# Newton-Schulz matrices turned by transposing DMA transfers in place of TensorE transposes, every third new X evicted by VectorE

## The chip, the cores and the metric

One core of a Trainium2 chip runs the whole program. The metric is the device time in microseconds (us) of one execution. TensorE (PE in the profile) multiplies and, in this kernel, also transposes; VectorE (DVE), ScalarE (ACT) and GpSimd (POOL) do the elementwise work, the first two also bring results out of PSUM; SyncE (SP) issues most DMA transfers.

## The reference, cut to what matters

A transformer layer on 8 batches of 256 tokens with 256 features: a modulated layer norm, an attention part whose three small weights per head are updated by one gradient step, and a mixture of 16 experts. The change is in the update. For each batch and each of two heads there are three 128x128 gradients, 48 matrices in all, and each is made nearly orthogonal by five Newton-Schulz steps in bf16:

```
def _zeropower_ns5(G):
    X = G.astype(jnp.bfloat16)
    nrm = jnp.linalg.norm(X.astype(jnp.float32).reshape(X.shape[0], -1), axis=1)
    X = X / (nrm[:, None, None].astype(jnp.bfloat16) + 1e-07)
    for a, b, c in NS_COEFFS:
        A = X @ jnp.swapaxes(X, 1, 2)
        Bm = b * A + c * (A @ A)
        X = a * X + Bm @ X
    return X.astype(jnp.float32)
```

The result is added to the gradient, its rows are scaled, and the sum is the weight with which the tokens' outputs are computed.

## The kernel before

Each engine has its own program, written out by hand in the order in which it runs; semaphores (`S[...]`) tell the engines of each other's progress, and a wait holds up everything behind it on its engine.

The 48 matrices lie in `X`, `[128, 48, 128]` bf16, and are taken in 12 groups of four (`NGRP`, `MPG`). Five steps over 12 groups make 60 turns, n = 0 to 59. A product X X^T needs the transposed X as TensorE's operand, so there is a second array `XT` of the same shape. The stage is a software pipeline, one loop over rounds r on each engine. In round r

- TensorE does A for turn r (L893, from `XT`), A A for turn r - 1 (L904, from `Ar`), the new X for turn r - 2 (L917 and L918, from `X`, `aI` and `Br`) and the transposes of the new X for turn r - 3 (L933);
- ScalarE evicts A scaled by b to `Ar` (L617) and the new X to `X` (L626);
- VectorE makes `Br` = b A + c A A (L1300) and copies the transposed matrices from PSUM to `XT` (L1306).

`Ar`, `Br` and the PSUM banks of A, A A, X and the transposes are two deep each. Turn n of one step and turn n + 12 of the next are the same group.

Before the first step there is no new X to turn. `first_turn(g)` (L857) transposes the 12 normalised groups on TensorE and `first_turned` (L571 on ScalarE for the even groups, L1263 on VectorE for the odd ones) copies them; groups 0 to 2 stand before the gradient products of the last batch, groups 3 to 5 behind them, and the rest in the rounds that `TURN_AT` names. The normalisation `x_init(b)` (L1257, L1259) of a batch's six matrices hangs on a chain: gradients out of PSUM (L578), cast to bf16 (L1251), sums of squares (L586, L1284, L1286), a sum over partitions on TensorE (L844), its copy (L566), a square root on GpSimd (L405, L407). For batch 7, the last, it stands in VectorE's round 6.

In the last step GpSimd adds each new X to its gradient (L460), TensorE transposes the sum (L949) and VectorE copies it (L1311).

SyncE starts the loads of the first five blocks of expert weights (`raw`, L329, two buffers) when the gradients are done; GpSimd splits each in two (L449, L451), beginning when all of `X` is normalised. From about 285 us on the mixture runs, in which nothing changes.

Of the kernel before, what the change touches and what calls it, by code (L numbers as in the profile page):

```python
# [27 lines left out]
P = 128  # L28
# [46 lines left out]
def build(nc, x_d, c_d, wmod_d, qkvw_d, w02_d, w1_d, wnat_d, wo_d, onw_d, gate_d, ident_d, moew_d, comb_d, out_d):  # L75
    ctx = ExitStack()
    with ctx:
# [149 lines left out]
        def bank(i):  # L227
# [16 lines left out]
            "f_ps", "f_sum", "f_norm", "f_b", "f_inv", "x_init", "t0_ps", "t0_a", "t0_v", "t_ps", "t_sb", "a_ps", "a_sb", "b_ps", "b_sb", "x_ps", "x_sb",  # L244
# [28 lines left out]
        def xt_ps(m):  # L273
            return bank(6 + m % 2).bitcast(BF16)[:, 0:BLK].rearrange("p (a d) -> p a d", d=P)

        FIRST_T = [4, 5, 2, 3, 4, 5, 6, 7, 6, 7, 6, 7]
        TURN_AT = {0: 6, 1: 7, 2: 8, 5: 9, 8: 10, 9: 11}

        def first_xt_ps(g):
            return bank(FIRST_T[g]).bitcast(BF16)[:, 0:BLK].rearrange("p (a d) -> p a d", d=P)  # L280
# [35 lines left out]
        def _(sp):  # L316
# [8 lines left out]
            sp.wait_ge(S["dw_ps"], B)  # L325
# [5 lines left out]
            for j in range(CPG):  # L331
                weights(j)
# [27 lines left out]
        def _(po):  # L360
# [96 lines left out]
            for g in range(NGRP):  # L457
                po.wait_ge(S["x_sb"], NGRP * (NS_STEPS - 1) + g + 1)
                wv = dw[:, g * MPG:(g + 1) * MPG, :]
                po.tensor_tensor(wv, wv, X[:, g * MPG:(g + 1) * MPG, :], ALU.add).then_inc(S["w_ok"], 1)  # L460
# [31 lines left out]
        def _(ac):  # L492
# [75 lines left out]
            def first_turned(g):  # L568

                ac.wait_ge(S["t0_ps"], g + 1)  # L570
                ac.activation(XT[:, g * MPG:(g + 1) * MPG, :], first_xt_ps(g), ACT.Copy).then_inc(S["t0_a"], 1)  # L571

# [32 lines left out]
            for g in (0, 2):  # L605
                first_turned(g)
# [3 lines left out]
            first_turned(4)  # L610
            for r in range(NGRP * NS_STEPS + 2):
# [6 lines left out]
                if TURN_AT.get(r - 1, 1) % 2 == 0:  # L618
                    first_turned(TURN_AT[r - 1])
# [92 lines left out]
        def _(pe_):  # L712
# [133 lines left out]
            def first_turn(g):  # L846

                pe_.wait_ge(S["x_init"], (4 * g + 3) // 6 + 1)
                for before in range(g):
                    if FIRST_T[before] == FIRST_T[g]:  # L850
                        pe_.wait_ge(S["t0_v" if before % 2 else "t0_a"], before // 2 + 1)
                if g == 6:
                    pe_.wait_ge(S["dw_sb"], NH * B)
                elif g >= 9:
                    pe_.wait_ge(S["t_sb"], {9: 2, 10: 5, 11: 6}[g])
                for a in range(MPG):
                    last = pe_.transpose(first_xt_ps(g)[:, a, :], X[:, g * MPG + a, :], identb[:, :])  # L857
                last.then_inc(S["t0_ps"], 1)

            pe_.wait_ge(S["const"], 7 + NS_STEPS)  # L860
            for b in range(1, B + 1):
# [7 lines left out]
                if b == B:  # L869
                    pe_.wait_ge(S["b_dg"], B)  # L870
                    for g in range(3):
                        first_turn(g)
# [3 lines left out]
            for g in range(3, 6):  # L876
                first_turn(g)
            NR = NGRP * NS_STEPS
            for r in range(NR + 4):
                n = r  # L880
                if n < NR:
                    g = n % NGRP
                    if n >= NGRP:
                        pe_.wait_ge(S["t_sb"], n + 1 - NGRP)
                    else:
                        pe_.wait_ge(S["t0_v" if n % 2 else "t0_a"], n // 2 + 1)
# [9 lines left out]
                if 0 <= n < NR:  # L896
# [3 lines left out]
                    else:  # L900
                        pe_.wait_ge(S["t0_v" if n else "t0_a"], 2)
# [5 lines left out]
                if 0 <= n < NR:  # L907
                    g = n % NGRP
                    pe_.wait_ge(S["b_sb"], n + 1)
                    if n >= 2:  # L910
                        pe_.wait_ge(S["x_sb"], n - 1)
                    else:
                        pe_.wait_ge(S["t0_v" if n else "t0_a"], 3)
# [6 lines left out]
                n = r - 3  # L920
                if 0 <= n < NR - NGRP:
                    g, m = n % NGRP, NGRP + n
                    pe_.wait_ge(S["x_sb"], n + 1)
                    if n >= 2:
                        pe_.wait_ge(S["t_sb"], n - 1)
                    if n in (0, 6):
                        pe_.wait_ge(S["t0_a"], 5 if n == 0 else 6)
                    elif n in (1, 3, 7):
                        if n == 1:
                            pe_.wait_ge(S["f_sum"], B)  # L930
                        pe_.wait_ge(S["t0_v"], {1: 4, 3: 5, 7: 6}[n])
                    for a in range(MPG):
                        last = pe_.transpose(xt_ps(m)[:, a, :], X[:, g * MPG + a, :], identb[:, :])  # L933
                    last.then_inc(S["t_ps"], 1)
                if r in TURN_AT:
                    first_turn(TURN_AT[r])
                if r == 2:
                    pe_.wait_ge(S["t0_v"], 4)
                    frob_sums(B - 1)
                n = r - 4  # L940
                if n >= NR - NGRP:
# [4 lines left out]
                    else:  # L946
                        pe_.wait_ge(S["t_sb"], NR - NGRP)
# [5 lines left out]
            pe_.wait_ge(S["x_sb"], NR)  # L953
# [131 lines left out]
        def _(ve):  # L1085
# [175 lines left out]
            def first_turned(g):  # L1261
                ve.wait_ge(S["t0_ps"], g + 1)
                ve.tensor_copy(XT[:, g * MPG:(g + 1) * MPG, :], first_xt_ps(g)).then_inc(S["t0_v"], 1)  # L1263

# [12 lines left out]
            first_turned(1)  # L1277
# [3 lines left out]
            first_turned(3)  # L1281
# [243 lines left out]
```

## Time and profile before

| | |
|---|---|
| runs | 711.73, 716.71, 719.69 us |
| median | 716.71 us |
| profiled execution | 712.38 us |
| its span in the trace | 710.6 us |
| mean granted TensorE clock | 0.983 |
| busy: PE, DVE, ACT, POOL | 94%, 68%, 49%, 30% of the span |

The span runs from the first instruction to the last one. A busy time is the sum over one engine's instructions; matmuls overlap, so the distance between the starts of two of them says more than the duration of one. In a timeline each row gives the start, the duration and the instruction, with its line, and in brackets the idle time before it and who ended that.

### The profile page before, as it was taken

What the parts mean: (1) busy time and instruction counts of PE and PEld (TensorE: products, weight loads), DVE (VectorE), ACT (ScalarE), POOL (GpSimd) and SP (SyncE); (2) the same over time, 40 slices, a digit from 0 to 9 for tenths busy, and PEclk for the clock granted to TensorE, in tenths of its full rate; (3) what the DMA queues carried; (4) which work ended last, traced back from release to release, by engine and by line L of the source; (5) the groups of instructions that cost most, each with busy time, mean ns of one, the idle gap of its engine ahead of it and who ended that gap; (6) DMA issues with size and microseconds to landing.
All of it is one profiled execution on the core that took longest, in us unless ns stands there. A gap on an engine that the chain in (4) does not pass through costs nothing.

```text
span 710.6 us, 11547 instructions
## 1 busy us (share of the span) xinstructions
PE 665.6 (94%) x4132; PEld 568.1 (80%) x4132; DVE 483.3 (68%) x960; ACT 345.2 (49%) x746; POOL 212.3 (30%) x210
## 2 busy tenths in 40 slices
PE   3998889779997899998999999999999999999997
PEld 3778779779995688887888888888888888888885
DVE  4788888999995478767545675665754766655555
ACT  3367669879998976453322323323223223223222
POOL 2255867944037664134100330013200331000000
PEclk9999999999998899999999999999999999999999
DMA  8000000021000000032003432243212432121223
GB/s 315 1 0 1 2 1 1 1 68 48 3 3 2 0 1 1 0 118 92 30 15 83 118 104 72 63 108 112 85 60 76 117 118 69 60 69 59 66 72 122
DMA packets 20472, 41.48 MB, mean 58 GB/s; under 512 B 3360, under 2 KB 3616, under 8 KB 20288
## 3 DMA queue, kind: packets, MB, share of 16 engines
q1 hardware_dynamic: 19392, 37.65, 17.2%
q10 hardware_dynamic: 832, 2.43, 1.0%
q8 instruction: 34, 0.56, 0.4%
q0 software_dynamic: 192, 0.66, 0.2%
q14 instruction: 22, 0.18, 0.1%
HBM read 38.50 MB, written 2.23 MB: 57 GB/s over the span
## 4 chain that ended last, share of the span: by engine, by line
PE 73%; ACT 9%; DVE 9%; POOL 3%; issue 3%; DMA 2%; ACTq 0%; DVEq 0%; POOLq 0%
PE ps L987 36%; PE ps L1058 18%; ACT junk L634 3%; PE ps L804 3%; PE ps L917 2%; PE ps L893 2%; PE ps L918 2%; PE ps L904 2%; PE ps L933 2%; DMA qkvw<-in_qkvw 1%; PE ps L834 1%; ACT junk L586 1%; PE ps L1005 1%; PE ps L1024 1%; DVE sq L1172 1%
## 5 line engine op out<-in xcount | busy, mean ns | idle before, releaser
L705 ACT ACTIVATE sgm<-ps,zero 128x512 f32<-128x512 f32 x100 | 68.9, 690 | 268.7 <-PE ps L987 268.7
L987 PE MATMUL ps<-h2hi,whi 128*128 128x512 f32 x400 | 156.1, 390 | 0.0
L987 PE MATMUL ps<-h2lo,whi 128*128 128x512 f32 x400 | 155.6, 389 | 0.0
L987 PE MATMUL ps<-h2hi,wlo 128*128 128x512 f32 x400 | 155.6, 389 | 0.0
L1466 DVE TENSOR_TENSOR am<-sgm,ps 128x512 f32<-128x512 f32 x88 | 60.6, 688 | 138.6 <-ACT sgm L705 138.5
L449 POOL CAST whi<-raw 128x768 fp32r<-128x768 f32 x25 | 22.4, 895 | 239.2 <-DMA raw<-in_moew 236.7
L987 PEld LDWEIGHTS ps<-h2lo,whi 128*128 128x128 f32 x400 | 75.1, 188 | 15.7
L987 PEld LDWEIGHTS ps<-h2hi,whi 128*128 128x128 f32 x400 | 75.1, 188 | 15.5
L987 PEld LDWEIGHTS ps<-h2hi,wlo 128*128 128x128 f32 x400 | 75.1, 188 | 15.4
L1058 PE MATMUL ps<-ahi,whi 128*128 128x512 f32 x200 | 77.9, 390 | 0.1
L1058 PE MATMUL ps<-alo,whi 128*128 128x512 f32 x200 | 77.8, 389 | 0.0
L1058 PE MATMUL ps<-ahi,wlo 128*128 128x512 f32 x200 | 77.8, 389 | 0.0
L1475 DVE TENSOR_TENSOR pm<-am,cw 128x512 f32<-128x512 f32 x88 | 72.2, 821 | 6.4 <-DMA cw<-combine 4.0
L1430 DVE TENSOR_TENSOR alo<-pm,ahi 128x512 fp32r<-128x512 f32 x100 | 75.7, 757 | 0.2
L695 ACT ACTIVATE ahi<-pm 128x512 fp32r<-128x512 f32 x100 | 62.3, 623 | 7.8 <-DVE pm L1468 5.0
L451 POOL TENSOR_TENSOR wlo<-raw,whi 128x768 fp32r<-128x768 f32 x25 | 47.9, 1917 | 2.0
L1058 PEld LDWEIGHTS ps<-ahi,whi 128*128 128x128 f32 x200 | 37.5, 188 | 8.3 <-DVE alo L1430 0.5
L1058 PEld LDWEIGHTS ps<-alo,whi 128*128 128x128 f32 x200 | 37.5, 188 | 7.8
L1058 PEld LDWEIGHTS ps<-ahi,wlo 128*128 128x128 f32 x200 | 37.5, 188 | 7.7
L1300 DVE SCALAR_TENSOR_TENSOR Br<-ps,Ar 128x512 bf16<-128x512 f32 x60 | 41.5, 691 | 2.5 <-PE ps L904 1.2
L617 ACT ACTIVATE Ar<-ps 128x512 bf16<-128x512 f32 x60 | 35.4, 593 | 4.1 <-PE ps L893 1.8
L626 ACT ACTIVATE X<-ps 128x512 bf16<-128x512 f32 x60 | 35.9, 598 | 3.1 <-PE ps L918 1.0
(206 smaller groups left out, 1238.5 us busy)
## 6 DMA issues: line engine op xcount, KB each, us to landing
raw<-in_moew SPq DMA_DIRECT2D x25, 384.0 KB, 3.8
cw<-combine SPq DMA_DIRECT2D x32, 256.0 KB, 3.2
cw<-combine SPq DMA_DIRECT2D x16, 224.0 KB, 3.0
cw<-combine SPq DMA_DIRECT2D x16, 192.0 KB, 2.9
cw<-combine SPq DMA_DIRECT2D x16, 160.0 KB, 2.7
cw<-combine SPq DMA_DIRECT2D x16, 128.0 KB, 3.0
out<-x1T SPq DMA_DIRECT2D x8, 256.0 KB, 3.7
cw<-combine SPq DMA_DIRECT2D x16, 96.0 KB, 2.8
```

The source lines that it names most:

```text
L449: po.tensor_copy(whi[wg % 2][:, c, :], raw[:, j % 2, :]).then_inc(S["w_hi"], 1)
L451: po.tensor_tensor(wlo[wg % 2][:, c, :], raw[:, j % 2, :], whi[wg % 2][:, c, :].bitcast(F32), ALU.subtract).then_inc(S["w_prep"], 1)
L617: ac.activation(Ar[:, n % 2, :], bank(n % 2), ACT.Copy, scale=NS[n // NGRP][1]).then_inc(S["a_sb"], 1)
L626: ac.activation(X[:, g * MPG:(g + 1) * MPG, :], bank(4 + n % 2).rearrange("p (a d) -> p a d", d=P), ACT.Copy).then_inc(S["x_sb"], 1)
L695: ac.activation(ahi[:, n % 4, :], pm[:, n % 3, :], ACT.Copy).then_inc(S["e_hi"], 1)
L705: ac.activation(sgm[:, n % 2, :], gate_bank(n), ACT.Silu, bias=zero[:, :]).then_inc(S["e_sg"], 1)
L987: last = mm(o, w_, a_[:, kc, tok], start=(kc == 0 and k == 0), stop=(kc == KC - 1 and k == 2))
L1058: last = mm(bank(6 + f), w_, a_, start=(c == 0 and k == 0), stop=(c == CPG - 1 and k == 2))
L1300: ve.scalar_tensor_tensor(out=Br[:, n % 2, :], in0=bank(2 + n % 2), scalar=c_ / (b_ * b_), in1=Ar[:, n % 2, :], op0=ALU.mult, op1=ALU.add) ...
L1430: ve.tensor_tensor(alo[:, n % 3, :], pm[:, n % 3, :], ahi[:, n % 4, :].bitcast(F32), ALU.subtract).then_inc(S["e_lo"], 1)
L1466: ve.tensor_tensor(am[:, n % 2, :], sgm[:, n % 2, :], lin_bank(n), ALU.mult).then_inc(S["e_a"], 1)
L1475: ve.tensor_tensor(pm[:, n % 3, :], am[:, n % 2, :], cw[:, k % 3, :], ALU.mult).then_inc(S["e_p"], 1)
```

## The change

The transposes of X leave TensorE, and their copies leave ScalarE and VectorE. SyncE issues, for each of the 60 turns, one transposing DMA transfer of a group from `X` to `XT`, 128 KB. Before it SyncE waits for the transfer four turns back, for the normalised X (first step) or for A of the turn 12 back and the eviction of its new X (later steps). TensorE waits for the transfer before A. The loads of the raw weights are issued between transfers 4, 8, 20, 24 and 28. In the first four steps the new X of every third turn is evicted by VectorE in place of ScalarE (`on_vector`); `evicted(n)` names the semaphore and count of turn n. The normalisations of batches 6 and 7 stand in VectorE's rounds 2 and 5 in place of 3 and 6.

```diff
+        NTURN = NGRP * NS_STEPS
+
+        def on_vector(n):
+            return n % 3 == 2 and n < NGRP * (NS_STEPS - 1)
+
+        def evicted(n):
+            if on_vector(n):
+                return S["x_sb_v"], sum(on_vector(k) for k in range(n + 1))
+            return S["x_sb_a"], sum(not on_vector(k) for k in range(n + 1))
+
+        def turned_in(m):
+            return S[f"xt_ld{m % 4}"], 16 * (m // 4 + 1)
...
-            sp.wait_ge(S["dw_ps"], B)
+            sp.wait_ge(S["dw_ps"], B - 1)
+            sp.wait_ge(S["b_dg"], B)
...
-            for j in range(CPG):
-                weights(j)
+            for m in range(NTURN):
+                g = m % NGRP
+                if m >= 4:
+                    sp.wait_ge(*turned_in(m - 4))
+                if m < NGRP:
+                    sp.wait_ge(S["x_init"], (4 * g + 3) // 6 + 1)
+                else:
+                    sp.wait_ge(S["a_ps"], m - NGRP + 1)
+                    sp.wait_ge(*evicted(m - NGRP))
+                sp.dma_start_transpose(XT[:, g * MPG:(g + 1) * MPG, :], X[:, g * MPG:(g + 1) * MPG, :]).then_inc(turned_in(m)[0], 16)
+                if m in (4, 8, 20, 24, 28):
+                    if m == 4:
+                        sp.wait_ge(S["dw_ps"], B)
+                    weights((4, 8, 20, 24, 28).index(m))
...
-                if n >= 0:
+                if n >= 0 and not on_vector(n):
                     g = n % NGRP
                     ac.wait_ge(S["x_ps"], n + 1)
                     ac.activation(X[:, g * MPG:(g + 1) * MPG, :], bank(4 + n % 2).rearrange("p (a d) -> p a d", d=P),
-                                  ACT.Copy).then_inc(S["x_sb"], 1)
+                                  ACT.Copy).then_inc(S["x_sb_a"], 1)
...
+                    pe_.wait_ge(*turned_in(n))
                     if n >= NGRP:
-                        pe_.wait_ge(S["t_sb"], n + 1 - NGRP)
+                        pe_.wait_ge(*evicted(n - NGRP))
...
-                n = r - 3
-                if 0 <= n < NR - NGRP:
-                    g, m = n % NGRP, NGRP + n
-                    pe_.wait_ge(S["x_sb"], n + 1)
-                    if n >= 2:
-                        pe_.wait_ge(S["t_sb"], n - 1)
...
-                    for a in range(MPG):
-                        last = pe_.transpose(xt_ps(m)[:, a, :], X[:, g * MPG + a, :], identb[:, :])
-                    last.then_inc(S["t_ps"], 1)
-                if r in TURN_AT:
-                    first_turn(TURN_AT[r])
...
-                if r in (3, 6):
-                    x_init(B - 2 if r == 3 else B - 1)
+                if r in (2, 5):
+                    x_init(B - 2 if r == 2 else B - 1)
...
-                n = r - 3
-                if 0 <= n < NR - NGRP:
-                    g, m = n % NGRP, NGRP + n
-                    ve.wait_ge(S["t_ps"], n + 1)
-                    ve.tensor_copy(XT[:, g * MPG:(g + 1) * MPG, :], xt_ps(m)).then_inc(S["t_sb"], 1)
+                n = r - 2
+                if 0 <= n < NR and on_vector(n):
+                    g = n % NGRP
+                    ve.wait_ge(S["x_ps"], n + 1)
+                    ve.tensor_copy(X[:, g * MPG:(g + 1) * MPG, :], bank(4 + n % 2).rearrange("p (a d) -> p a d", d=P)).then_inc(S["x_sb_v"], 1)
```

How it moves SyncE's queue, from the last load of the start on (`gatew`, the router's weights). Before:

```order
7 L323 DMA gatew<-in_gate 128x32
8 L329 DMA raw<-in_moew 128x768 [waits dw_ps]
9 L329 DMA raw<-in_moew 128x768
10 L329 DMA raw<-in_moew 128x768 [waits w_prep] x3
11 L339 DMA combine<-combT 16x1024 [waits combT_ok]
```

And of the change, up to the first transfer of the second step:

```order
7 L327 DMA gatew<-in_gate 128x32
8 L345 DMA_TRANSPOSE XT<-X 128x4x128 [waits x_init,b_dg,dw_ps]
9 L345 DMA_TRANSPOSE XT<-X 128x4x128 [waits x_init] x3
10 L345 DMA_TRANSPOSE XT<-X 128x4x128 [waits x_init,xt_ld0]
11 L334 DMA raw<-in_moew 128x768 [waits dw_ps]
12 L345 DMA_TRANSPOSE XT<-X 128x4x128 [waits x_init,xt_ld1]
13 L345 DMA_TRANSPOSE XT<-X 128x4x128 [waits x_init,xt_ld2]
14 L345 DMA_TRANSPOSE XT<-X 128x4x128 [waits x_init,xt_ld3]
15 L345 DMA_TRANSPOSE XT<-X 128x4x128 [waits x_init,xt_ld0]
16 L334 DMA raw<-in_moew 128x768
```

The first load of raw weights now has five transfers before it in the queue, and the second nine.

VectorE at the start of the stage, from the first Br. Before:

```order
215 L1300 SCALAR_TENSOR_TENSOR Br<-ps,Ar 128x512 [waits b_ps]
216 L1263 COPY XT<-ps 128x512 [waits t0_ps]
217 L1300 SCALAR_TENSOR_TENSOR Br<-ps,Ar 128x512 [waits b_ps]
218 L1257 RECIPROCAL finv<-fnb 128x6 [waits f_b]
219 L1259 TENSOR_TENSOR X<-X,finv 128x768 [waits f_inv]
220 L1300 SCALAR_TENSOR_TENSOR Br<-ps,Ar 128x512 [waits x_ps,b_ps]
221 L1306 COPY XT<-ps 128x512 [waits t_ps]
```

And of the change, from the same place into the steady part:

```order
212 L1260 SCALAR_TENSOR_TENSOR Br<-ps,Ar 128x512 [waits b_ps]
213 L1226 RECIPROCAL finv<-fnb 128x6 [waits f_b]
214 L1228 TENSOR_TENSOR X<-X,finv 128x768 [waits f_inv]
215 L1260 SCALAR_TENSOR_TENSOR Br<-ps,Ar 128x512 [waits b_ps]
216 L1260 SCALAR_TENSOR_TENSOR Br<-ps,Ar 128x512 [waits x_ps,b_ps] x2
217 L1266 CAST X<-ps 128x512 [waits x_ps]
218 L1226 RECIPROCAL finv<-fnb 128x6 [waits f_b]
219 L1228 TENSOR_TENSOR X<-X,finv 128x768 [waits f_inv]
220 L1260 SCALAR_TENSOR_TENSOR Br<-ps,Ar 128x512 [waits x_ps,b_ps] x3
221 L1266 CAST X<-ps 128x512 [waits x_ps]
```

The copies to `XT` are gone, the scaling of batch 6 stands before the second Br, and one eviction of X (CAST) stands behind every third Br.

## Rows read from the trace of the kernel before

**Rows 1.** The page, busy time, share of the span and instructions of each engine.

```profile
PE 665.6 (94%) x4132; PEld 568.1 (80%) x4132; DVE 483.3 (68%) x960; ACT 345.2 (49%) x746; POOL 212.3 (30%) x210
```

**Rows 2.** Stretches: from:to, length, busy time (instructions) by engine, PEclk, DMA.

```profile
137.00:143.60 6.60, 5.95 (x49) 5.76 (x50) 5.85 (x12) 4.90 (x17) 4.81 (x6) 0.74 0.01 2
...
159.30:205.00 45.70, 45.70 (x823) 45.70 (x821) 44.77 (x83) 43.95 (x81) 7.99 (x7) 1.00 0.08 20
```

**Rows 3.** Groups of instructions by line, whole span: busy us, mean ns, idle before.

```profile
L1306 DVE COPY XT<-ps 128x512 bf16<-128x512 bf16 x48 | 20.3, 424 | 1.1 <-PE ps L933 1.1
...
L933 PE MATMUL ps<-identb,X 128*128 128x128 bf16 x192 | 18.5, 219 | 2.1 <-ACT XT L571 1.2 <-DVE XT L1263 0.9
...
L460 POOL TENSOR_TENSOR dw<-dw,X 128x512 f32<-128x512 f32 x12 | 13.7, 1160 | 38.2 <-ACT X L626 38.1
```

**Rows 4.** Timeline of PE, one steady round: start, duration, instruction.

```profile
161.56 0.39 PE L893 MATMUL ps<-XT 128*128 128x128 bf16 x4
...
162.45 0.39 PE L933 MATMUL ps<-identb,X 128*128 128x128 bf16 x4
162.67 0.39 PE L893 MATMUL ps<-XT 128*128 128x128 bf16 x4
162.90 0.39 PE L904 MATMUL ps<-Ar 128*128 128x128 bf16 x4
```

**Rows 5.** Timelines of ACT and DVE, the same round.

```profile
161.53 0.60 ACT L626 ACTIVATE X<-ps 128x512 bf16<-128x512 f32 x1
162.03 0.59 ACT L617 ACTIVATE Ar<-ps 128x512 bf16<-128x512 f32 x1
162.65 0.60 ACT L626 ACTIVATE X<-ps 128x512 bf16<-128x512 f32 x1
...
163.32 0.69 DVE L1300 SCALAR_TENSOR_TENSOR Br<-ps,Ar 128x512 bf16<-128x512 f32 x1
```

**Rows 6.** Timeline of PE, end of the stage.

```profile
205.10 0.39 PE L893 MATMUL ps<-XT 128*128 128x128 bf16 x4
...
206.00 0.39 PE L893 MATMUL ps<-XT 128*128 128x128 bf16 x4
...
212.81 0.39 PE L893 MATMUL ps<-XT 128*128 128x128 bf16 x4
...
215.48 0.39 PE L893 MATMUL ps<-XT 128*128 128x128 bf16 x4
```

**Rows 7.** Timelines of PE, DVE and POOL, start of the stage.

```profile
137.60 1.46 PE L857 MATMUL ps<-identb,X 128*128 128x128 bf16 x12 [1.22 <-DVE dgb L1272]
...
150.47 0.22 PE L917 MATMUL ps<-X,aI 128*128 128x128 bf16 x1
...
159.32 0.39 PE L893 MATMUL ps<-XT 128*128 128x128 bf16 x4
...
143.76 0.55 DVE L1251 CAST X<-dw 128x768 bf16<-128x768 f32 x1
...
146.21 0.42 DVE L1263 COPY XT<-ps 128x512 bf16<-128x512 bf16 x1
146.54 0.68 DVE L1300 SCALAR_TENSOR_TENSOR Br<-ps,Ar 128x512 bf16<-128x512 f32 x1
...
148.28 0.96 DVE L1259 TENSOR_TENSOR X<-X,finv 128x768 bf16<-128x768 bf16 x1
...
149.81 1.35 POOL L405 TENSOR_TENSOR fnb<-fsum,half 128x6 bf16<-128x6 f32 x1 [3.96 <-ACT fsum L566]
151.25 0.24 POOL L407 TENSOR_SCALAR fnb<-fnb 128x6 bf16<-128x6 bf16 x1
```

**Rows 8.** The page, DMA issues: count, KB each, median us from issue to landing.

```profile
combine<-combT SPq DMA_DIRECT2D x2, 64.0 KB, 2.3
```

**Rows 9.** Timeline of SyncE's queue: start, time to issue.

```profile
142.74 0.81 SPq L329 DMA_DIRECT2D raw<-in_moew  x2
...
304.16 0.34 SPq L339 DMA_DIRECT2D combine<-combT  x1
```

**Rows 10.** DMA queues from 1.4 to 2.6 us: packets, MB, share of 16 engines.

```profile
q1 hardware_dynamic: 144, 0.01, 7.1%
```

**Rows 11.** The same from 16.5 to 17.6 us.

```profile
q1 hardware_dynamic: 312, 0.18, 54.0%
```

More of the change, by code:

```diff
@@ L242, in build @@
             "xb_ok", "f_ss", "g_sq", "f_s7",
-            "f_ps", "f_sum", "f_norm", "f_b", "f_inv", "x_init", "t0_ps", "t0_a", "t0_v", "t_ps", "t_sb", "a_ps", "a_sb", "b_ps", "b_sb", "x_ps", "x_sb",
+            "f_ps", "f_sum", "f_norm", "f_b", "f_inv", "x_init", "xt_ld0", "xt_ld1", "xt_ld2", "xt_ld3", "a_ps", "a_sb", "b_ps", "b_sb", "x_ps", "x_sb_a", "x_sb_v",
             "w_ok", "wt_ps", "wt_sb", "rss_ok", "ws_chain", "w_scale",
@@ L457, in _ @@
             for g in range(NGRP):
-                po.wait_ge(S["x_sb"], NGRP * (NS_STEPS - 1) + g + 1)
+                po.wait_ge(*evicted(NGRP * (NS_STEPS - 1) + g))
                 wv = dw[:, g * MPG:(g + 1) * MPG, :]
@@ L566, in sum_out @@
                 ac.activation(fsum[:, 6 * b:6 * b + 6], frob_ps(b), ACT.Copy).then_inc(S["f_sum"], 1)
-            def first_turned(g):
-                ac.wait_ge(S["t0_ps"], g + 1)
-                ac.activation(XT[:, g * MPG:(g + 1) * MPG, :], first_xt_ps(g), ACT.Copy).then_inc(S["t0_a"], 1)
             def grads_out(b):
@@ L604, in _ @@
             sum_out(B - 3)
-            for g in (0, 2):
-                first_turned(g)
             grad_squares(B - 2)
@@ L844, in frob_sums @@
                 mm(frob_ps(b), ones[:, :], fss[:, 6 * b:6 * b + 6], start=True, stop=True).then_inc(S["f_ps"], 1)
[L846 to L855, printed above, removed]
-                for a in range(MPG):
-                    last = pe_.transpose(first_xt_ps(g)[:, a, :], X[:, g * MPG + a, :], identb[:, :])
-                last.then_inc(S["t0_ps"], 1)
             pe_.wait_ge(S["const"], 7 + NS_STEPS)
@@ L870, in _ @@
                     pe_.wait_ge(S["b_dg"], B)
-                    for g in range(3):
-                        first_turn(g)
                     pe_.wait_ge(S["f_sum"], B - 2)
@@ L875, in _ @@
             frob_sums(B - 2)
-            for g in range(3, 6):
-                first_turn(g)
             NR = NGRP * NS_STEPS
@@ L910, in _ @@
                     if n >= 2:
-                        pe_.wait_ge(S["x_sb"], n - 1)
-                    else:
-                        pe_.wait_ge(S["t0_v" if n else "t0_a"], 3)
+                        pe_.wait_ge(*evicted(n - 2))
                     for a in range(MPG):
@@ L919, in _ @@
                     last.then_inc(S["x_ps"], 1)
-                n = r - 3
-                if 0 <= n < NR - NGRP:
-                    g, m = n % NGRP, NGRP + n
-                    pe_.wait_ge(S["x_sb"], n + 1)
-                    if n >= 2:
-                        pe_.wait_ge(S["t_sb"], n - 1)
[L926 to L932, printed above, removed]
-                        last = pe_.transpose(xt_ps(m)[:, a, :], X[:, g * MPG + a, :], identb[:, :])
-                    last.then_inc(S["t_ps"], 1)
-                if r in TURN_AT:
-                    first_turn(TURN_AT[r])
                 if r == 2:
-                    pe_.wait_ge(S["t0_v"], 4)
+                    pe_.wait_ge(S["dw_sb"], NH * B)
                     frob_sums(B - 1)
@@ L946, in _ @@
                     else:
-                        pe_.wait_ge(S["t_sb"], NR - NGRP)
+                        pe_.wait_ge(S["f_sum"], B)
                     for a in range(MPG):
@@ L950, in _ @@
                     last.then_inc(S["wt_ps"], 1)
-            pe_.wait_ge(S["x_sb"], NR)
+            pe_.wait_ge(*evicted(NR - 1))
             pe_.wait_ge(S["wt_sb"], NGRP)
@@ L1280, in _ @@
             x_init(B - 3)
-            first_turned(3)
             cast_grads(B - 1)
```

20 lines of the change are left out of this document (1 added, 19 removed).

## The prediction, made before the changed kernel ran

> **What bounds the kernel now.** I read the busy times first: TensorE (PE) is busy 94% of the 710.6 us [rows 1], so only what shortens PE's own sequence, or the waits in it, can pay. Then the table of stretches, for the place that the change touches: the Newton-Schulz stage runs from 143.6 to 219 us. In its steady part PE is busy for the whole 45.70 us, but VectorE (DVE) has 44.77 and ScalarE (ACT) 43.95 of the same stretch [rows 2]. Three engines are nearly full at once, so what comes off PE alone is not the gain.
>
> Then the timeline of one steady round, a round being one turn of the loop over 60 groups of four matrices. The product A = X X^T of one round starts at 161.56, the next at 162.67: the round takes 1.115 us [rows 4]. It has 20 matmuls 0.056 us apart: four transposes (L933), four for A (L893), four for A A (L904), eight for the new X (L917, L918). PE never waits in it.
>
> **What the change takes away in a steady round.** The four transposes start at 162.45 and the next group follows at 162.67: 0.22 us of PE per group, for the 48 groups of L933 [rows 3, 4]. VectorE's copies of the turned matrices go too, 48 of 424 ns [rows 3]. Every third new X moves from ScalarE (about 0.60 us each, row of 162.65 [rows 5]) to VectorE. The trace has no VectorE copy of this kind; the nearest row is its own operation Br, also 128x512 fp32 from PSUM to bf16, 0.69 us [rows 5]. I take 0.69. PE's sum for a round becomes 1.115 - 0.22 = 0.89 us. The row that shows such a round: the first one after the last transposes runs from 205.10 to 206.00, 0.90 us [rows 6].
>
> **Why the round won't become 0.89.** The buffers are two deep and the chain between the engines takes over. ScalarE evicts X and A in turns. An X eviction starts 0.20 us after the next group on PE does (162.45 to 162.65), and ScalarE's following operation starts no less than 0.50 us after it (161.53 to 162.03) [rows 4, 5]. So in the new order the eviction of A starts 0.70 after A's first matmul, runs 0.59 and hands over in about 0.05: A A can start at 1.34. PE would be there after one whole round and the four matmuls of the next A, at 0.89 + 0.22 = 1.11. The stall s counts twice on the way, once in each round: 1.11 + 2s = 1.34, s = 0.115, round = 1.005 us. Where VectorE takes X, ScalarE is free and this stall goes, but Br then waits for that copy (it would start at 0.20 + 0.60 = 0.80 instead of 0.22 + 0.42 = 0.64, the 0.42 from 162.90 to 163.32 [rows 4, 5]). It ends at 1.49 and the next X is late by about 0.2. So the third that is moved exchanges one stall for another of the same size. I take 1.00 us for a round, with 0.89 and 1.06 as its ends: the sum of PE alone, and both stalls in full in every third round. From round 10 (159.32) to the last with a transpose there are 41 rounds: 41 x (1.115 - 1.00) = 4.7 us.
>
> **The start of the stage.** Today the first 12 groups are turned by PE too (L857), twelve matmuls of them, 1.46 us from 137.60, ahead of the last gradient products [rows 7]. The transfers take their place beside the gradients. Part of that gain is lost, since PE begins cold there (granted clock 0.74 from 137 to 143.6, nearer to the lower level than what follows at 1.00 [rows 2]) and the gradients take over the slow matmuls: I take 0.9. The cast at 143.76, on which the last batch's norm hangs, moves up with it, and one copy (0.42 us each, 0.34 from start to start) between it and the first Br goes: Br at 145.3 instead of 146.54 [rows 7]. The scaling of batch 6 now stands a round earlier, in front of the second Br (0.96 us for the product that starts at 148.28, 1.15 with its reciprocal; it delayed the third Br before). By this the third X product starts at about 148.6 instead of 150.47, 1.9 us earlier [rows 7]. The scaling of batch 7 hangs on GpSimd, which starts its power at 149.81 now, 1.35 and 0.24 us long; it would start at 148.4, and 1.35 + 0.24 + 1.15 later, at 151.1, VectorE would go on. Then four rounds of 1.00 to round 10 at 155.3, against 159.32: 4.0 us in all [rows 7]. The last two transfers of the first pass leave at 151.1 and have four rounds to land.
>
> **The end.** For the last 12 groups PE has transposes of the sum (L949): 1.34 us a round (two from 212.81 to 215.48), with an addition of 1.16 on GpSimd [rows 3, 6]. Nothing there gets shorter or longer, since no X goes to VectorE in that step. The loads of raw weights that move between the transfers feed GpSimd's split, which now ends near 169; the latest would be issued by round 18 or so, near 163, as now. I cost them at nothing: the first user of the weights starts at 285.5 us.
>
> **What the transfers cost.** 60 of 128 KB each, SBUF to SBUF, on SyncE's queue, at most four in flight. There is none in the trace. Three prices are wanted.
> - Landing. The nearest row, 64 KB out of SBUF, lands in 2.3 us [rows 8]; with twice the bytes I allow 3.2. From X's eviction to the A that needs the transfer are 12 - 3 = 9 rounds, 9 us: hidden, unless it lands later than 9 us. But four in flight give one in landing / 4: 0.58 to 0.80 us, below 1.00. It begins to cost at 4 us.
> - The engines' time. If the rows of 256 bytes are packets of their own, there are 512. Small packets took 7.1% of 16 engines' 1.2 us over 144 of them, 9.5 ns each [rows 10], and 54.0% of 1.1 us over 312, 30 ns, these of about 580 bytes [rows 11]. Between them by size, some 20 ns: 512 x 20 / 16 = 0.64 us a group, 0.30 at 9.5 and 0.96 at 30.
> - The issue. SyncE takes 0.34 us for a plain one [rows 9].
>
> I take 0.64, which is below the round, so transfers cost the path nothing. Their upper end is from the same rows: four in flight and 30 ns gives 0.96, still covered; if a transfer holds the stream until it has landed, 2.3 us, it is not. With an interval I above 1.1 us the stream sets the end: 60 I + 2 us from 137.6, against 215.5 today for the last A [rows 6], a change of 60 I - 76 us. It breaks even near 1.27.
>
> **Sum.** 4.7 + 4.0 = 8.7 us off the profiled execution's 712.38 us: 703.7. That execution stands 4.3 below the median of 716.71, whose runs lie between 711.73 and 719.69; on the median's scale 708.
>
> **Rivals.**
> 1. *The stream of transfers is slower than the rounds.* Nothing in the trace shows how fast SyncE issues a transposing transfer or the engines move one. At I = 1.5 us the change is 60 x 1.5 - 76 = +14, 726 (731 on the median's scale); at 2.0 +44, 756 (761). For it: all prices above are of plain transfers. Against it: even the 30 ns packet leaves 0.96. It decides from 1.27 on; chance 0.21. The Trainium skill, "DMA: Bandwidth & Descriptors", in the table of transposes before the fast path, counts 262,144 sequencer cycles for 8,192 tiles from SBUF to SBUF, one push per tile; the X-bar section of the same page takes 16 partitions by 128 elements as one tile. By it the 32 tiles of a group are 1,024 cycles, an estimate of 0.85 us at 1.2 GHz ahead of any fixed part, and the sum stays as it is only if that part is under 0.3 us. No row here shows it.
> 2. *Transfers pass one after the other*, each occupying the stream for its whole landing time. With the 2.3 us of [rows 8]: 60 x 2.3 - 76 = +62, 774 (779). For it: no row shows two transposing transfers under way together. Against it: plain ones do overlap, as the two raw loads issued at 142.74 and 0.4 us later [rows 9]. Chance 0.16. The Trainium skill, "VectorE: DVE Perf Modes", section "The three transpose paths", gives 1309 ns for one 128x128 matrix by DMA against 390 on TensorE; four in a row would be an estimate of 5.2 us a group and 240 us lost. The same skill's "DMA: Bandwidth & Descriptors", section "Latency and other measured facts", has 261 GB/s for such transfers, 0.50 us a group, and would leave my sum.
> 3. *Nearly even*: an interval between 1.1 and 1.3, from landing in 4.5 to 5 us with four in flight or from issue. The gain of the start stays, that of the rounds goes: 60 x 1.2 - 76 = -4, to +2; about 709 to 714 (713 to 719). Chance 0.15.
> 4. The forecast, 0.48. Within it the change can do less than it says, because the round falls to 1.06 and not to 1.00 (41 x 0.06 = 2.5 less); that leaves 6 us, under 1%: 0.10 of the 0.48.
>
> One per cent is 7.2 us, about what the spread of the runs lets one tell. So faster 0.38, within 1% 0.10 + 0.15 = 0.25, slower 0.21 + 0.16 = 0.37. The range: 41 rounds at 0.95 and two us more at the start give about 703 on the median's scale, a low run 699. Its upper end takes in rival 1 to I = 2.0, 760, and leaves out rival 2. If the forecast's mechanism holds, its own range is 699 to 712.
>
> **What would show it.** The distance of two A products in the steady part: 1.00 confirms the chain, 0.89 says that I overcharged it, 1.2 or more with PE idle before A and a transfer as its releaser is rival 1. Their time to landing tells rival 2 (I = landing / 4 when they overlap, I = landing when not). The first Br near 145.3 and round 10 near 155.3 confirm the start. My sum is wrong if PE's idle time before A names a transfer anywhere after round 10.

## The result, and the profile after

The change makes the kernel slower: 729.44 us (median of 4, 727.66 to 732.53) against 714.22 (4, 711.43 to 719.69) in the same session, ratio 1.021 (1.018 to 1.025). The forecast was 708. The profiled execution has a span of 727.6 us against 710.6, 17.0 more. Measured on one scale, from the end of the last gradient product on VectorE to the last product A, the Newton-Schulz stage takes 92.5 us (139.5 to 232.0) instead of 77.9 (137.6 to 215.5): 14.6 of the 17.0. Another 1.9 is a later begin of the stage in code that the change doesn't touch. That begin lies between 137.3 and 143.8 us from one profiled run to another, also in kernels with the same code up to there, so the experiments below are compared by the length of the stage as well as by total time. A length comes from one profiled execution and is itself good to about 1.5 us: two runs below whose streams hold the same transfers and loads differ from the changed kernel by 1.0 and 1.4.

The stretches of the changed kernel, with the columns of [rows 2]:

```profile
137.00:143.60 6.60, 4.40 (x20) 4.37 (x21) 5.62 (x10) 4.00 (x17) 6.36 (x6) 0.58 0.22 44
143.60:160.00 16.40, 13.45 (x152) 12.28 (x151) 12.49 (x20) 9.29 (x19) 7.68 (x9) 0.75 0.90 128
160.00:200.00 40.00, 29.20 (x435) 25.79 (x432) 23.93 (x37) 25.69 (x47) 9.18 (x7) 0.96 0.67 117
200.00:232.00 32.00, 25.47 (x381) 22.70 (x382) 21.30 (x34) 23.08 (x40) 9.04 (x8) 1.00 0.54 92
```

Where [rows 2] has three engines full in the steady part, none is: PE is busy 29.2 of 40 us, VectorE 23.9, ScalarE 25.7, and the DMA engines 0.67. The page of the profile says what PE waits for; its groups have the columns of [rows 3]. The first line is the chain of work that ended last: 7% of the span runs through SyncE's queue (SPq), which had no part in it before:

```profile
PE 68%; ACT 8%; DVE 7%; SPq 7%; POOL 3%; issue 3%; DMA 3%; ACTq 0%; DVEq 0%; POOLq 0%
...
L883 PE MATMUL ps<-XT 128*128 128x128 bf16 x240 | 24.7, 228 | 17.9 <-DMA XT<-X 17.0
```

PE stands idle 17.9 us before A (L883), 17.0 of them for a transfer from `X` to `XT`. The prediction said that its sum is wrong if just this is seen. The products A on PE's timeline, to be held against [rows 4]:

```profile
196.16 0.40 PE L883 MATMUL ps<-XT 128*128 128x128 bf16 x4 [0.39 <-DMA XT<-X]
197.54 0.40 PE L883 MATMUL ps<-XT 128*128 128x128 bf16 x4 [0.31 <-DMA XT<-X]
198.86 0.40 PE L883 MATMUL ps<-XT 128*128 128x128 bf16 x4 [0.26 <-DMA XT<-X]
200.16 0.40 PE L883 MATMUL ps<-XT 128*128 128x128 bf16 x4 [0.23 <-DMA XT<-X]
201.44 0.40 PE L883 MATMUL ps<-XT 128*128 128x128 bf16 x4 [0.22 <-DMA XT<-X]
202.77 0.40 PE L883 MATMUL ps<-XT 128*128 128x128 bf16 x4 [0.26 <-DMA XT<-X]
```

A round takes 1.31 us, not 1.00 and not 1.115, and each A is released by a transfer. What sets the 1.31 stands on the timeline of SyncE's queue (start, time to issue):

```profile
196.38 1.21 SPq L345 DMA_TRANSPOSE XT<-X  x1
197.69 1.21 SPq L345 DMA_TRANSPOSE XT<-X  x1
...
202.93 1.92 SPq L345 DMA_TRANSPOSE XT<-X  x1
...
212.81 1.75 SPq L345 DMA_TRANSPOSE XT<-X  x1
...
222.51 2.13 SPq L345 DMA_TRANSPOSE XT<-X  x1
```

SyncE needs 1.21 us to issue one transposing transfer and 0.10 more to the next: 1.31. The plain transfer that the prediction took as its price needs 0.34 [rows 9]. Landing is not the limit. From 196 to 200 us the view of the queues gives

```profile
q1 hardware_dynamic: 1632, 0.39, 48.4%
...
XT<-X SPq DMA_TRANSPOSE x4, 2.4
```

that is 2.4 us to land (median), and 1,632 packets, three transfers of 544. They took 48.4% of 16 engines' 4 us, 19 ns a packet. Over the whole stage the median to land is 2.5 us; two transfers are under way at once.

**The 89.1 us of the stream.** The first issue is at 139.54, the last of 60 at 228.67. 59 intervals of 1.31 are 77.3; five loads of raw weights stand between them, 4.4; one wait for the scaling of batch 7, 1.3; and eight issues take 1.6 to 2.2 us instead of 1.21 (three are shown), which makes 6.1 with a gap of 0.5 us that follows one of them. Together 89.1. The last A is 3.3 us behind the last issue. So the stage ends when the stream ends, and it is late by the stream's four parts.

### The profile page after: what moved, and what is told of

Same layout as the page of the kernel before. It is cut to its first block, busy times and chain, and to the rows that moved or that the text cites. A ratio compares the mean times of both kernels' runs of the same rounds, so it can differ in the third digit from the quotient of the medians.

```text
span 727.6 us, 11064 instructions
## 1 busy us (share of the span) xinstructions
PE 664.8 (91%) x3892; PEld 561.0 (77%) x3892; DVE 471.4 (65%) x922; ACT 336.1 (46%) x724; POOL 212.2 (29%) x210
## 3 DMA queue, kind: packets, MB, share of 16 engines
q10 hardware_dynamic: 832, 2.43, 1.0%
## 4 chain that ended last, share of the span: by engine, by line
PE 68%; ACT 8%; DVE 7%; SPq 7%; POOL 3%; issue 3%; DMA 3%; ACTq 0%; DVEq 0%; POOLq 0%
PE ps L956 37%; PE ps L1027 18%; SPq L345 7%; ACT junk L641 2%; PE ps L811 2%; PE ps L841 2%; DMA qkvw<-in_qkvw 1%; PE ps L993 1%; ACT junk L598 1%; DMA XT<-X 1%; PE ps L974 1%; DVE x L1375 1%; PE ps L767 1%; DVE sq L1141 1%; DVE qk L1115 1%
## 5 line engine op out<-in xcount | busy, mean ns | idle before, releaser
L1027 PE MATMUL ps<-ahi,whi 128*128 128x512 f32 x200 | 77.9, 390 | 0.1
L883 PE MATMUL ps<-XT 128*128 128x128 bf16 x240 | 24.7, 228 | 17.9 <-DMA XT<-X 17.0
```

The lines of the kernel that those rows point to most:

```text
L883: last = mm(bank(n % 2)[:, a * P:(a + 1) * P], XTm, XTm, start=True, stop=True)
L1027: last = mm(bank(6 + f), w_, a_, start=(c == 0 and k == 0), stop=(c == CPG - 1 and k == 2))
```

## The experiments

Each is a change of the changed kernel if nothing else is said. "Interval" is the distance of two issues on SyncE, "stage" the length as defined above (before 77.9, changed 92.5). A ratio is to the kernel before, with its 95% interval.

### What sets the interval: the transfers in flight, their bytes, or the issue

**Eight in flight.** There are four more semaphores, and SyncE waits for the transfer eight back instead of four.

```
-            return S[f"xt_ld{m % 4}"], 16 * (m // 4 + 1)
+            return S[f"xt_ld{m % 8}"], 16 * (m // 8 + 1)
...
-                if m >= 4:
-                    sp.wait_ge(*turned_in(m - 4))
+                if m >= 8:
+                    sp.wait_ge(*turned_in(m - 8))
```

> Transfers may run eight deep in place of four. Theory A (SyncE's issue of a transposing transfer, 1.21 us and 0.10 between two, sets the interval): nothing changes, 1.31 us between two issues in the steady part, 726 to 732 us. Rival B (landing time with four in flight, 2.5 us and up to 5.0): the stops in the queue go, and the time falls by 5 to 10 us, to 719 to 725.

730.56 us, 1.024 (1.015 to 1.032); stage 91.1. The interval stays where it was:

```profile
191.08 1.21 SPq L345 DMA_TRANSPOSE XT<-X  x1
192.39 1.21 SPq L345 DMA_TRANSPOSE XT<-X  x1
```

The number of transfers in flight is not the limit.

**The same bytes without the turn.** The 48 later transfers are plain copies to a spare tile `XD`. A reads what the 12 first turns left, so the products are of stale matrices.

```
+                if m < NGRP:
+                    sp.dma_start_transpose(XT[...], X[...])...
+                else:
+                    sp.dma_start(XD[:, m % 4 * MPG:(m % 4 + 1) * MPG, :], X[...])...
...
```

> From the second step on the 48 transfers are plain copies of the same 128 KB from SBUF to SBUF into a ring of four, waited for in the same way, and A is made from the matrices turned for the first step (later steps don't use their own transposed X). Theory A: the issue falls to 0.3 to 0.6 us, the interval is set by the rounds (about 1.0 us), and the time is 708 to 714 us. Rival C (what costs is 128 KB through the DMA engines from SBUF to SBUF, or the chain of waits A, eviction, transfer, A): the interval stays at 1.3 and the time near 729.

711.99 us in the one run, where the kernel before has a median of 715.19 (9 runs); stage 72.5. SyncE takes 0.46 to 0.55 us for 42 of the 48 and 1.0 to 2.1 for six (the distance below is set by the rounds now):

```profile
191.41 0.52 SPq L349 DMA_DIRECT2D XD<-X  x1
192.57 0.46 SPq L349 DMA_DIRECT2D XD<-X  x1
```

and the rounds take 1.04 on average. As many transfers with as many bytes and the same waits are hidden as soon as they don't transpose.

**Half the bytes.** Each transfer turns two of its four matrices, and A uses each of them twice, so half of the products are of the wrong matrix.

```
-  sp.dma_start_transpose(XT[:, g * MPG:(g + 1) * MPG, :], X[:, g * MPG:(g + 1) * MPG, :])
+  sp.dma_start_transpose(XT[:, g * MPG:g * MPG + 2, :], X[:, g * MPG:g * MPG + 2, :])
...
-                        XTm = XT[:, g * MPG + a, :]
+                        XTm = XT[:, g * MPG + a % 2, :]
```

> Each transfer turns two of a group's four matrices, and A uses these two twice (the other two A are left out). If an issue has a fixed price (A1): still 1.2 to 1.3 us each, 726 to 732 us. If the price goes with the bytes or blocks (A2): about 0.65 to 0.75 us an issue, less than a round, and 706 to 713 us.

727.06 us, 1.019 (1.010 to 1.027); stage 89.1:

```profile
192.04 1.17 SPq L345 DMA_TRANSPOSE XT<-X  x1
193.31 1.19 SPq L345 DMA_TRANSPOSE XT<-X  x1
```

Half the bytes, almost the same issue. So the price is one per transfer, and nearly none per byte.

**Twice the bytes, half the transfers.** 30 transfers of two groups (256 KB), which each wait for the second group's eviction.

```
-            for m in range(NTURN):
+            for k in range(NTURN // 2):
+                m = 2 * k
...
-  sp.dma_start_transpose(XT[:, g * MPG:(g + 1) * MPG, :], X[:, g * MPG:(g + 1) * MPG, :])
+  sp.dma_start_transpose(XT[:, g * MPG:(g + 2) * MPG, :], X[:, g * MPG:(g + 2) * MPG, :])
```

> 30 transfers of eight matrices in place of 60 of four. A1 (fixed price per issue): 30 issues of 1.3 us, hidden, 706 to 713 us. A2 (price by blocks): 2.4 us an issue, 30 gaps of 0.10 saved, and a later start of each pair: 725 to 733 us.

709.45 us (8 runs), 0.992 (0.989 to 0.995); stage 73.9, 4.0 shorter than before and 18.6 shorter than in the changed kernel.

```profile
187.56 1.23 SPq L347 DMA_TRANSPOSE XT<-X  x1
189.58 1.23 SPq L347 DMA_TRANSPOSE XT<-X  x1
```

Twice the bytes, 1.23 us to issue: the sizes 64, 128 and 256 KB give medians of 1.19, 1.21 and 1.23. The rounds pace the stream, and from 160 to 200 us PE's weight loads wait for a transfer once (the view of waits: us in all, times, the longest):

```profile
PEld ps L885 <- DMA XT<-X: 1.2, 1, 1.2
```

This one edit turns the loss into a gain, which shows the cause of the largest part. No run issued the transfers from another engine, so whether part of the price is SyncE's own is open.

### The other parts of the stream

**The raw weights from GpSimd's own queue.** Takes the five loads out of SyncE's stream.

```
-                if m in (4, 8, 20, 24, 28):
-                    ...
-                    weights((4, 8, 20, 24, 28).index(m))
...
+            def load_raw(j):
+                ...
+                po.dma_start(raw[:, j % 2, :], moew_d[:, j, :]).then_inc(S[f"ld_rp{j % 2}"], 16)
...
```

> The five loads of raw weights leave SyncE's queue: GpSimd issues them itself. Theory A (everything that SyncE issues adds up, since its queue is the bottleneck): 60 transfers stay 1.31 us apart, and the 4.4 us that the loads take between them (0.6 to 1.8 each) come off: ratio to before 1.013 to 1.017 in place of 1.021. Rival (the loads hide in the queue's waits, or cost by traffic on the DMA engines, which stays): no change, 1.019 to 1.025.

726.65 us, 1.018 (1.014 to 1.023); stage 90.7. Of 4.4 us only 1.9 come back, between what the two expectations say. Long issues took a part of the rest: those at 156.28, 168.00 and 175.01 us take 2.43, 2.47 and 2.09. The loads' 4.4 is what they occupy in the stream; that taking them out is worth 4.4 was not shown, and 1.9 is hardly more than the 1.4 by which "eight in flight" was shorter with all loads in place.

**One wait less.** SyncE doesn't wait for A's signal, since X's eviction implies it.

```
-                    sp.wait_ge(S["a_ps"], m - NGRP + 1)
```

> The changed kernel without SyncE's wait for A before each later transfer (the eviction of the new X, which comes after that A, is still waited for): one instruction less per transfer in SyncE's queue. If the price of an issue were in the waits, the interval of 1.31 us would fall by about 0.1 and the time by 5 us; if it is the transposing transfer's own, it stays at 1.30 to 1.31. The long issues (1.6 to 2.4 us, every seventh or eighth) come at wider spacing if they go with the number of instructions read, at the same if with time or transfers. Total 724 to 731 us.

729.31 us, 1.020 (1.015 to 1.024), stage 91.5, interval 1.31, and the long issues at the same distance of about 10 us. The 0.10 between two issues is not that wait.

**The long issues.** In the changed kernel the queue of instructions q8 moves nine packets of 16 KB from 137 to 232 us (count, MB, share):

```profile
q8 instruction: 9, 0.15, 0.7%
```

Read in windows of half a microsecond, the first eight lie at 149.0, 159.0, 167.5, 178.0, 190.5, 202.5, 212.5 and 222.0 us, and SyncE's long issues start at 149.41, 158.50, 167.58, 178.31 (a raw load, 1.77 us instead of 0.57), 191.31, 202.93, 212.81 and 222.51. (The eighth long transfer of the sum above, 1.58 us at 164.59, has its packet on the other queue of instructions, q14, at 164.0; the raw load's excess is in the 4.4.) The distance of about 10 us could be that of PE's instructions, of which it has 32 a round (16 matmuls and 16 weight loads), far more than any other engine. Two edits change their number. First, two matrices share one matmul of 256 columns, so PE has the same columns with half the instructions (half of the products are then of a matrix with its neighbour):

```
-                    for a in range(MPG):
-                        XTm = XT[:, g * MPG + a, :]
-                        last = mm(bank(n % 2)[:, a * P:(a + 1) * P], XTm, XTm, start=True, stop=True)
+                    for a in range(0, MPG, 2):
+                        last = mm(bank(n % 2)[:, a * P:(a + 2) * P], XT[:, g * MPG + a, :],
+                                  XT[:, g * MPG + a:g * MPG + a + 2, :]..., start=True, stop=True)
...
```

> Asked: where the long issues of the transfers come from (eight of 1.6 to 2.2 us in the changed kernel instead of 1.21, 6.1 us in all). In the changed kernel each of these eight has a transfer of instructions on queue q8 (one packet of 16 KB) in the same half microsecond, 149.0 to 222.0 us, nine to twelve us apart; the three on q14 go with shorter delays. Here two matrices share one matmul of 256 columns in A, A A and the new X: the same columns on TensorE, half the instructions (8 matmuls and 8 weight loads a round instead of 16 and 16). Half of the products are of one matrix with its neighbour, so the output is not the reference's. If the long issues come with the fetch of TensorE's instructions: four or five of them with q8, twice as far apart, the stage about 3 us shorter, ratio to the kernel before about 1.017 (1.012 to 1.019). If they belong to the transfers themselves (every seventh or eighth issue, whatever TensorE does): eight again at the same distance, ratio 1.021 (1.018 to 1.025).

726.45 us, 1.017 (1.013 to 1.020); stage 90.0, 2.5 shorter. The interval of the ratio overlaps with the changed kernel's (1.018 to 1.025), and equal streams differ by 1.4, so these two numbers don't decide. The trace does. It has five packets on q8 in the same stretch instead of nine:

```profile
q8 instruction: 5, 0.08, 0.4%
```

and the long issues in the late part are 18 us apart instead of 10:

```profile
182.04 2.09 SPq L345 DMA_TRANSPOSE XT<-X  x1
...
200.37 2.13 SPq L345 DMA_TRANSPOSE XT<-X  x1
...
218.33 2.38 SPq L345 DMA_TRANSPOSE XT<-X  x1
```

All five go with a packet on q8 (147.5, 162.0, 182.0, 200.0, 218.0), and one of 1.54 us at 166.77 with one on q14 (167.0). Second, the other way, each product A A is computed twice, 20 matmuls and 20 weight loads a round:

```
+                        mm(bank(2 + n % 2)[:, a * P:(a + 1) * P], Am, Am, start=True, stop=True)
                         last = mm(bank(2 + n % 2)[:, a * P:(a + 1) * P], Am, Am, start=True, stop=True)
```

> The other direction: each product of A A is computed twice into the same place, with the same result: 20 matmuls and 20 weight loads a round instead of 16 and 16, TensorE's own round 1.11 us, still below the 1.31 us of the transfers. If the long issues come with the fetch of TensorE's instructions: ten of them with q8 instead of eight, about 7.5 to 9 us apart, the stage 1 to 2 us longer, ratio about 1.023 (1.020 to 1.027). If they belong to the transfers: eight, ratio 1.021.

730.00 us, 1.020 (1.018 to 1.023); stage 94.0, 1.5 longer. Neither the total nor the 1.5 separates the two expectations. The trace does: ten packets on q8,

```profile
q8 instruction: 10, 0.16, 0.8%
```

and ten long issues, each beside one of the ten packets; in the late part they start at 196.66, 203.79, 210.73, 218.06 and 229.35, four of them 7 us apart and the last 11. So a fetch of PE's instructions lengthens the issue that runs beside it, by 0.4 to 1.5 us in these runs (1.6 to 2.7 in place of 1.21). It is no property of the transposing transfer: in the kernel with plain copies the six that take 1.0 to 2.1 us instead of 0.46 to 0.55 all run beside a packet on q8. Why a fetch does this isn't shown.

### The rounds and the start, apart from the stream

**Turned once, ScalarE alone.** Only the 12 first transfers; later products A read the stale `XT`. Every new X is evicted by ScalarE.

```
-            return n % 3 == 2 and n < NGRP * (NS_STEPS - 1)
+            return False
...
-            for m in range(NTURN):
+            for m in range(NGRP):
...
```

> Only the 12 transfers of the first step, later A are made from the matrices turned then (steps 2 to 5 don't turn their X), and all X are evicted by ScalarE. It shows the round without any turning: by the chain of the prediction 1.00 us, by PE's sum 0.89, and if the third that VectorE takes is what makes the 1.04 us of the plain copies possible, 1.06 to 1.12. Total by the first 708 to 712 us, ratio 0.99 to 0.997.

709.21 us (10 runs), 0.993 (0.990 to 0.995); stage 71.7; rounds of 0.98 and 1.04 in turns, 1.01. This is what the stage is worth with no stream at all behind the start: 6.2 us. The forecast wanted 8.7.

**Half by DMA.** The kernel before, with its own start; later turns of odd number by a transposing transfer, the others by PE and VectorE, every X on ScalarE.

```
+            for n in range(1, NGRP * (NS_STEPS - 1), 2):
+                ...
+                sp.dma_start_transpose(XT[:, g * MPG:(g + 1) * MPG, :], X[:, g * MPG:(g + 1) * MPG, :])...
```

> The kernel before with its start, and of the 48 later turns every second one by a transposing transfer, every other one by PE and VectorE as before; all X on ScalarE. Theory A: 24 issues of 1.31 us in 48 rounds are hidden, PE's sum is 1.00 on average, the chain gives about 1.04 to 1.06 a round: 3 us less than before, ratio 0.994 to 0.998. Rival (a transfer that lands late or a chain that binds at each change between the two ways): 1.00 to 1.01.

710.75 us (10 runs), 0.994 (0.991 to 0.997); stage 74.2; rounds of 0.89 and 1.18, 1.04 on average. At one transfer in two rounds the same transfers of 128 KB are hidden.

**VectorE's third alone.** The kernel before, with every third X evicted by VectorE and no transfers.

```
-                if n >= 0:
+                if n >= 0 and not on_vector(n):
...
+                n = r - 2
+                if 0 <= n < NR and on_vector(n):
+                    ve.tensor_copy(X[...], bank(4 + n % 2)...).then_inc(S["x_sb_v"], 1)
```

> The kernel before with only one part of the change: every third X evicted by VectorE. VectorE then has 0.60 (Br) + 0.36 (XT) + 0.20 (a third of an X) = 1.16 us a round against 1.115: slower by 2 us in the 48 rounds, ratio 1.001 to 1.006. Rival (ScalarE was what set the round): faster, 0.99 to 0.998.

720.03 us (10 runs), 1.005 (1.002 to 1.009); stage 81.9, 4.0 longer than before. Two rounds of 1.12 and one of 1.37. VectorE in such a round:

```profile
178.25 0.69 DVE L1308 SCALAR_TENSOR_TENSOR Br<-ps,Ar 128x512 bf16<-128x512 f32 x1
178.85 0.68 DVE L1314 CAST X<-ps 128x512 bf16<-128x512 f32 x1
179.45 0.41 DVE L1319 COPY XT<-ps 128x512 bf16<-128x512 bf16 x1
```

The copy of X (0.68; 0.69 was predicted) delays what stands behind it. The part on VectorE, put into the kernel before, is a loss by itself.

**Eight matrices and ScalarE alone**, the version that the runs point to: the edits of "twice the bytes" and `return False` together.

> 30 transfers of eight matrices as before, and no X on VectorE. The rounds of the kernel that turned once were 1.01 us with all X on ScalarE, those with eight matrices and a third on VectorE 1.04: 39 rounds x 0.03 = 1.2 us less than e4, ratio to the kernel before 0.988 to 0.992. Rival (ScalarE needs the relief as soon as transfers run beside it, since X comes later into the transfers): 0.992 to 1.0.

707.99 us (6 runs, 704.42 to 713.64), 0.990 (0.986 to 0.994); stage 72.7. It is the fastest by its median, and beats both kernels; to the 709.45 of the version with VectorE's third the intervals overlap.

```profile
160.00:200.00 40.00, 39.88 (x634) 35.26 (x632) 27.18 (x40) 40.00 (x80) 7.91 (x6) 1.00 1.04 164
```

The queues in the same 40 us (packets, MB, share of 16 engines):

```profile
q1 hardware_dynamic: 21727, 6.46, 103.4%
```

ScalarE is busy for all 40.00 us, with two evictions a round, and sets the round of 1.01 us. The DMA engines' share is 1.04. Whether that is a second limit isn't shown: the rounds are the same 0.98 and 1.04 as in the kernel that has no transfers there, and a share over 1 means that the times of packets overlap.

**The first step by fours, then by eights.** As the last, with 12 single transfers at the start.

> The first step's 12 groups by single transfers of four matrices with no load of raw weights among the first ten, then 24 transfers of eight, all X on ScalarE. A transfer of four lands in 2.5 us and not in 3.5 or more, so the A of turn 10 comes 1 us sooner than in e10; ratio 0.986 to 0.991. Rival (the start is set by the 1.31 us an issue of single transfers, 12 x 1.31 = 15.7 us): up to 2 us slower than e10, 0.991 to 0.995.

710.54 us (6 runs), 0.993 (0.990 to 0.995), which misses what the theory wanted in total and lies in the rival's range. The stage is 72.0, of it 19.1 to round 10, where the kernel before has 21.8 and the one with eights at the start 20.7. But its profiled execution entered the stage at 142.8, 5.5 later than the last kernel's, in code that is the same. Totals can't tell these two versions apart.

## Why the prediction was wrong

| from the end of the gradients, us | before | changed | expected gain | measured gain |
|---|---|---|---|---|
| to round 10 | 21.8 | 20.5 | 4.0 | 1.2 |
| round 10 to 51 | 45.8 | 59.8 | 4.7 | -14.0 |
| round 51 to 59 | 10.4 | 12.2 | 0 | -1.8 |

**The step that failed is the issue of a transposing transfer.** The prediction put it at SyncE's 0.34 us "for a plain one"; it is 1.21 and 0.10. Landing (0.58 to 0.80 us a transfer) and the engines' time (0.30 to 0.96) were bounded from both sides. For the issue one row stood for both ends, and it was of another kind of transfer. So the step "transfers cost the path nothing" fell with it: the interval is 1.31, not 0.64, and longer than the round. Rival 1 names the mechanism (PE idle before A, a transfer as its releaser), and the measured 1.31 lies beyond its point of decision, 1.27. Its formula 60 I - 76 gives only +3 there, where the stage lost 14.6. It took the stream as transfers alone. What lay between them was worth more than the excess over 1.27: the raw loads 4.4, the scaling 1.3, the long issues 6.1. The prediction costs the raw loads at nothing, since their user comes at 285.5 us; but they cost their place in a queue that had become the bound.

**Landing and the engines were right.** Expected were 3.2 us to land, measured 2.5 over the stage (2.4 from 196 to 200 us). Expected were 512 packets of 20 ns and 0.64 us a group, measured 544 of 19 ns: 544 x 19 / 16 = 0.65. With eights and ScalarE alone the 21,343 small packets took 27.6 ns on average from 160 to 200 us, which makes 0.94 us a group, just inside the forecast's upper end (0.96). Rival 2 falls: transfers that take 2.4 us to land leave every 1.31.

**The chain's round was right.** 1.00 was predicted. Free of the stream it is 1.01 with ScalarE alone and 1.04 with VectorE's third. "Exchanges one stall for another of the same size" was too kind by 0.03 us a round, and in the kernel before, where VectorE also has the copies, by 0.08.

**The start was too large in its size, and the issue had a part in that too.** Counted from the end of the gradients, the first Br was to come at 7.8 us (145.3), against 9.0 before. In the changed kernel it comes at 9.0 (148.47), no earlier. The granted clock goes with this. Two stretches of 6 us from the end of the gradients, of the changed kernel and of "the raw weights from GpSimd's own queue", whose code is the same up to there:

```profile
139.46:145.46 6.00, 5.76 (x30) 5.62 (x30) 4.89 (x10) 3.33 (x13) 4.23 (x5) 0.55 0.43 87
137.51:143.51 6.00, 5.32 (x36) 4.94 (x37) 5.27 (x10) 4.46 (x17) 4.76 (x6) 0.72 0.43 87
```

The second has 0.72, as the kernel before has, and its first Br at 8.0. Of the twelve runs with the changed start eight have 0.72 here and the first Br at 8.0 to 8.2, and four have 0.50 to 0.57 and 8.9 to 9.1. So 1.0 of the expected 1.2 us is there when the clock is as before, and is lost when it is lower. No edit set the clock, so this is a comparison of executions. From 143.6 to 160 us the changed kernel was granted 0.75, between the lower level (1.2 GHz) and the full one (2.4 GHz), where the kernel before had the full one (1.00) from 6 us behind its end of the gradients on. That doesn't explain round 10: "eight in flight" and "one wait less" had 1.00 from 6 to 22 us behind the end of the gradients, and reached it at 20.4 and 20.5, as the changed kernel did (20.5).

What they share is the stream. The prediction let the last two transfers of the first pass leave at 151.1, 13.6 us behind the end of the gradients. Ten intervals of 1.31 and two loads of 0.63 before the first of the two are 14.4 by themselves; it left at 15.6 to 16.4 in the three kernels named, and in "eight in flight" PE waits for a transfer ahead of round 9:

```profile
163.25 0.40 PE L883 MATMUL ps<-XT 128*128 128x128 bf16 x4 [1.93 <-DMA XT<-X]
```

The kernels with the changed start reach round 10 after 18.9 to 21.1 us, 0.7 to 2.9 less than before; none gained the predicted 4.0. How much of the rest is the clock's, the scaling's and the stream's isn't separated.

**The end.** Nothing was expected. Round 51 to 59 takes 1.8 more because the last transfers are still late: A of turn 54 waits for its own until 225.28. Where the stream is hidden the same rounds take 10.6.

**Rules and rows.** The Trainium skill's "DMA: Bandwidth & Descriptors", by its one push per tile in the table of transposes before the fast path, gave an estimate of 0.85 us for the 32 tiles of a group. By that rule 64 and 256 KB would cost half and twice as much; they cost 1.19 and 1.23. The measurement decides: the rule is too low by 0.36 us at 128 KB, and wrong in form. The 261 GB/s of the same page of the Trainium skill, section "Latency and other measured facts", would be an estimate of 0.50 us a group; the stream moved 128 KB in 1.31 us, 100 GB/s, and with eights in 1.0 us, 130 GB/s. The Trainium skill's "VectorE: DVE Perf Modes", section "The three transpose paths", has 1309 ns for one matrix. Four of them don't pass one after the other at that price, an estimate of 5.2 us, since four land in 2.4 us.

**Sums.** Two small slips change nothing: 151.1 and four rounds of 1.00 make 155.1 and not 155.3, and the low end of the forecast, 4 us under 708, is 704 and not 703.

The total of 729.4 lies inside the range of 699 to 760 only because that range was stretched over rival 1 up to an interval of 2.0. At the measured 1.31 that rival's formula gives about 719 on the median's scale, so the total is inside by the width of the range and not by its reckoning.

## What to carry over

When work is moved to a DMA queue, price three things apart for this kind of transfer: landing, the engines' time, and the issue on the queue's own engine. Where the trace shows only another kind, the issue needs two ends like the others. Then add up the queue's whole stream, with what else stands in it, and hold it against the rounds. If the issue has a fixed price, halving the number of transfers is worth more than anything that makes each smaller or deeper in flight.

## What the runs showed of the hardware

- Issuing a transposing transfer from SBUF to SBUF on SyncE took 1.19, 1.21 and 1.23 us (medians) for 64, 128 and 256 KB; a plain copy of 128 KB took 0.46 to 0.55 where no fetch of instructions ran beside it.
- An issue of 128 KB beside a fetch of TensorE's instructions (16 KB on q8) took 1.6 to 2.7 us, and a plain copy's 1.0 to 2.1. From 137 to 232 us nine such fetches became five with half as many instructions, and ten with a quarter more.
- Packets of 256 bytes took 19 ns where the DMA engines' share was 0.48, and 27.6 ns where it was 1.04.
- In the first 6 us of the stage the granted clock was 0.72 in eight executions with the changed start and 0.50 to 0.57 in four, and the first Br came 1 us later in the four.
